# Spreading the four indirect transfers of a block over events of the turn, and holding the gathers of two phases to four blocks ahead

## The reference

```python
x = layernorm(x + gcn(x, src, dst, ...))        # two convolutions, 64 -> 128 -> 64
x = layernorm(x + attention(x, src, dst, ...))  # softmax over the edges of a target
x = layernorm(x + relations(x, edge_attr_64, edge_type_10, src, dst, ...))  # tanh scores, softmax
x = layernorm(x + messages(x, src, dst, edge_attr_32, ...))  # two MLPs
# e.g. attention:
#   e = gelu(s_src[src] + s_dst[dst]);  a = softmax of e over the edges of one dst
#   h = segment_sum(a * z[src], dst) + (x @ res_W + res_b)
```

## Time and profile before

| | us |
|---|---|
| median of 3 runs | 6235.68 |
| lowest, highest | 6197.13, 6236.36 |
| the profiled execution, its own time | 6214.3 |
| its span, first to last instruction | 6212.5 |

### The profile page before, as it was taken

The page is one execution under the profiler, slowest core; times in us unless marked ns, Lnnn a source line. Parts: engine busy times, 40 slices in busy tenths (PEclk is TensorE's granted clock), DMA queues, the critical chain, the costliest instruction groups (busy, mean ns, idle before and its releaser), DMA issues. The chain is left out here.

```text
span 6212.5 us, 80161 instructions
## 1 busy us (share of the span) xinstructions
PE 5134.0 (83%) x25341; PEld 3285.1 (53%) x25341; DVE 3278.3 (53%) x6838; ACT 1898.0 (31%) x3531; POOL 2770.6 (45%) x2859
## 2 busy tenths in 40 slices
PE   6899988888889999727888789999999877777776
PEld 1266666666667676604555545555555534444443
DVE  9755555555544444526555467777777622222222
ACT  0055554333333333301111114444444311111111
POOL 0144443545544444463542153433332056666665
PEclk9899998899989999956565598888888677777777
DMA  1177776666754454323332243333333122222221
GB/s 31 37 214 218 221 221 190 165 167 174 177 147 136 129 138 133 102 54 82 90 87 73 58 101 82 91 87 90 86 86 78 29 67 54 53 46 52 54 54 24
DMA packets 1124519, 649.11 MB, mean 104 GB/s; under 512 B 907542, under 2 KB 940589, under 8 KB 1124104
## 3 DMA queue, kind: packets, MB, share of 16 engines
q1 hardware_dynamic: 1036296, 555.84, 33.0%
q0 software_dynamic: 87808, 88.16, 7.1%
HBM read 384.69 MB, written 261.63 MB: 104 GB/s over the span
## 5 line engine op out<-in xcount | busy, mean ns | idle before, releaser
L1047 POOL DMA_INDIRECT o_rows<-in_x_dram,dst_idx x392 | 370.0, 944 | 661.8 <-POOLq L347 265.9
L1488 POOL DMA_INDIRECT b_rows<-h_table,slot_idx x392 | 369.8, 943 | 440.9 <-DVE n_res L1021 318.9
L2591 DVE TENSOR_TENSOR_SCAN m_both<-m_keep,m_both,m_rows_t 128x512 f32<-128x512 bf16 x97 | 124.2, 1280 | 815.0 <-remote 458.1
L2464 POOL DMA_INDIRECT out_dram<-s_res,put_out x392 | 390.4, 996 | 352.6 <-DVE s_res L1241 223.9
L1931 POOL DMA_INDIRECT t_got<-x_table,slot_idx x392 | 370.8, 946 | 383.9 <-DVE t_rows L2041 239.7
L1305 POOL DMA_INDIRECT a_got<-node_table,src_idx x392 | 372.0, 949 | 368.5 <-DVE n_res L1021 214.2
L1201 ACT ACTIVATE s_square<-s_sum_t 128x256 f32<-128x256 f32 x392 | 149.2, 381 | 1232.6 <-remote 580.3
L2245 PE MATMUL r_source_t<-r_masked,rel_pair 64*128 64x512 f32 x980 | 523.0, 684 | 0.0
L2247 PE MATMUL r_own_t<-r_masked,rel_pair 64*128 64x512 f32 x980 | 522.8, 684 | 0.0
L1007 DVE TENSOR_REDUCE n_power<-n_square 128x8 f32<-128x512 f32 x294 | 200.9, 683 | 604.9 <-ACT n_square L982 312.0
L2146 POOL DMA_INDIRECT r_got<-x_table,slot_idx x392 | 382.4, 976 | 297.8 <-POOLq L1920 183.0
(11 more groups left out here) (390 smaller groups left out, 13082.2 us busy)
## 6 DMA issues: line engine op xcount, KB each, us to landing
x_table<-n_res SPq DMA_DIRECT2D x196, 256.0 KB
n_rows<-x_table SPq DMA_DIRECT2D x196, 256.0 KB
x_table<-s_res SPq DMA_DIRECT2D x294, 128.0 KB
node_table<-n_wide SPq DMA_DIRECT2D x98, 272.0 KB
h_table<-n_conv SPq DMA_DIRECT2D x98, 256.0 KB
x_table<-s_res SPq DMA_DIRECT2D x98, 256.0 KB
r_feats<-in_edge_attr_dram SPq DMA_DIRECT2D x390, 64.0 KB
n_rows<-in_x_dram SPq DMA_DIRECT2D x97, 256.0 KB
```

The source lines that it names most:

```text
L1047: nc.gpsimd.indirect_dma_start(out=rows[:, n % 4, t, :], out_offset=None, in_=x, in_offset=bass.IndirectOffsetOnAxis(ap=dst_idx[:, n * TIL ...
L1488: nc.gpsimd.indirect_dma_start(out=rows[:, n % 4, t, 0:D], out_offset=None, in_=h_table, in_offset=bass.IndirectOffsetOnAxis(ap=slot_idx[: ...
L2464: nc.gpsimd.indirect_dma_start(out=out, out_offset=bass.IndirectOffsetOnAxis(ap=put_out[:, n * TILES + t:n * TILES + t + 1], axis=0), in_= ...
```

## The change

In the first five phases each of a block's four gathers now waits for an event of its own. In the attention and relation phases `gather(n)` also waits for `scanned[n - 4]` before its first transfer, so that it no longer runs ahead over the whole ring. Nothing is computed otherwise, and the number of transfers is the same.

```diff
 own_phase, gather(n), in the loop over t:
-                            if t == TILES // 2 and n >= 5:
+                            if t == 1 and n >= 8:
+                                pool.wait_ge(fed.powered[n - 8], fed.powered.done(n - 8))
+                            if t == 2 and n >= 8:
+                                pool.wait_ge(fed.ready[n - 8], fed.ready.done(n - 8))
+                            if t == 3 and n >= 5:
                                 pool.wait_ge(nodes.ready[n - 5], nodes.ready.done(n - 5))
 first_conv_phase:
-                            if t == TILES // 2 and n >= 5:
+                            if t == 1 and n >= 6:
+                                pool.wait_ge(conv_made[n - 6], conv_made.done(n - 6))
+                            if t == 2 and n >= 5:
                                 pool.wait_ge(nodes.ready[n - 5], nodes.ready.done(n - 5))
+                            if t == 3 and n >= 4:
+                                pool.wait_ge(scanned[n - 4], scanned.done(n - 4))
 second_conv_phase:
-                            if t == TILES // 2 and n >= 4:
+                            if t == 1 and n >= 4:
+                                pool.wait_ge(nodes.powered[n - 4], nodes.powered.done(n - 4))
+                            if t == 2 and n >= 4:
                                 pool.wait_ge(nodes.ready[n - 4], nodes.ready.done(n - 4))
+                            if t == 3 and n >= 4:
+                                pool.wait_ge(norm.ready[n - 4], norm.ready.done(n - 4))
 attention_phase:
+                        if n >= 4:
+                            pool.wait_ge(scanned[n - 4], scanned.done(n - 4))
                         for t in range(TILES):
+                            if t == 1 and n >= 4:
+                                pool.wait_ge(source_matched[n - 4], source_matched.done(n - 4))
+                            if t == 2 and n >= 4:
+                                pool.wait_ge(score_kept[n - 4], score_kept.done(n - 4))
+                            if t == 3 and n >= 4:
+                                pool.wait_ge(turned[n - 3], turned.done(n - 3))
 relation_phase:
+                        if n >= 4:
+                            pool.wait_ge(scanned[n - 4], scanned.done(n - 4))
                         for t in range(TILES):
+                            if t == 1 and n >= 4:
+                                pool.wait_ge(masks_made[n - 4], masks_made.part(n - 4, 1))
+                            if t == 2 and n >= 4:
+                                pool.wait_ge(masks_made[n - 4], masks_made.done(n - 4))
```

## The result

The changed kernel takes 5974.94 us (median of 4 runs, 5966.95 to 5996.67), the kernel before 6218.20 us beside it (4 runs, 6197.13 to 6236.36): a ratio of 0.9631, with a 95% interval of 0.9599 to 0.9663. The forecast was 6180 with a range down to 6085; the kernel gained 243 us where 56 were forecast. The profiled execution has a span of 5980.8 us against 6212.5.

What follows compares the result with a forecast made beforehand. It took PE to bound own phase, convolutions and relations, and PE's signals, late during POOL's long gather runs, to hold attention. Gains of 45 + 6 + 5 = 56 us gave 6180 from 6235.7; 8 in 10 between 6085 and 6255.

Steps and rivals of the forecast that it cites:

- The reading: All phases: while POOL issues many gathers back to back, PE's finished work reaches others late, some 21 us at attention's start.
- The first rival: Attention's start: the late signal has nothing to do with POOL's run, the change only reorders POOL; 6236 us, chance 0.17.
- own phase and convolutions: First three phases: gathers stay nearly one run of four in an undisturbed turn; counted as 0 for all three.
- the runs of eight: Eight gathers of POOL in one run: expected rarer in attention, about as frequent in the first convolution.
- the sum: Whole kernel: 45 + 6 + 5 = 56 us off, from a median of 6235.7 to 6180, 0.9% faster.
- Attention, start: Up to block 28: POOL tied to the turn, turns of 6.0 us between 5.0 and 7.0; 45 us gained, 20 to 70.
- my own list: Signs in the changed profile; wrong would be, among others, turns of 7 us and more at attention's start.
- Attention, later: Rest of attention: the fourth gather's wait stops runs of two blocks; 6 us gained, between 0 and 18.
- Relations: Relations: first run about 22 gathers instead of 28, 5 us gained; later product hidden by 3.3 us slack, early turns 0.
- Small gaps are enough: First convolution: single gathers with any gap never delay PE's signals, 118 us more gained; 6062 us, chance 0.20.
- The long pause is what counts: Second convolution: cutting POOL's 3.3 us pause into pieces costs 108 us, turns above 8.3 us; 6288 us, chance 0.13.

Runs made afterwards that it cites:

- the probe: Kernel before; in attention's first 12 turns ACT makes a one-column activation as it sees each of four signals (rows landed, PE's work counted); 6209.59 us.
- the pause experiments: Kernel before with POOL memsets of different lengths between indirect transfers; the 128x256 one, about 0.2 us more per transfer, took 5897.46 us, ratio 0.9593.
- e3_parts: Kernel before with the change's waits in own phase, waits for long past events in first convolution, only the scanned[n - 4] hold in attention and relations; ratio 0.9765.
- the pauses: Kernel before with its own waits and a POOL memset of 128x512 between a block's transfers, in attention and relations before every transfer; 5856.72 us, ratio 0.9486.
- the two runs of 903 and 974 us: Changed kernel with all events awaited before a block's first transfer (ratio 1.018); kernel before with a 128x512 memset pause after every second transfer (1.0051).
- g2_pairs: Kernel before with a POOL memset of 128x512 only after every second indirect transfer, message phase included; 6238.23 us, ratio 1.0051.

## Why the prediction was wrong

**The reading was right, as far as it went.** "While POOL issues many gathers back to back, what PE has finished reaches the others late": the probe shows it with PE's two kinds of signal, and pausing POOL alone removes it. The first rival, that the late signal has nothing to do with the run, is out.

**The step that failed** is that of own phase and convolutions: the four events of a turn are "each little more than the 1.24 us apart that POOL needs for one. So in an undisturbed turn it is still nearly one run of four", and hence 0. The term measured 82 us in own phase, 44 in the first convolution and 8 in the second. The sentence was worked out for the first convolution and carried over to own phase unread. In own phase it is false: 144 gathers stand alone and 16 runs of four are left of 55, and 66 increments in place of 183 are over 1 us late. I asked whether the run becomes much looser, not how loose it has to be. Little is enough: 0.35 to 0.95 us between the gathers in the changed own phase, and in the pause experiments 0.2 us more from transfer to transfer in the message phase. For own phase the change's waits alone give it (715), and without the spread it is gone (821). In the first convolution the sentence is nearly true: half of the distances within a block are 1.29 us or less, and as many signals are late as before. What did change is that the runs of eight, which I had said stay, went from 11 to 1 and those of six from 11 to 35, and that the longest delays are rarer. How much of the 44 us that explains is not shown; waits that never wait gave 20 there (e3_parts). I had also looked for the disturbance only in the first convolution; for own phase, with PE busy for 717 of 803 us, I called the turn PE's and looked no further. 86 idle us, at a clock below full, were all to be had: with the pauses 12 are left.

**The clock was missing from the sum.** I had priced a late signal as waiting time. In own phase 38 of the 82 us are matmuls that became shorter (717 to 679 busy, clock 0.91 to 0.95). That less waiting brings a higher clock is no rule, though: in the second convolution the change brought idle time down from 75 to 33 us and busy time up from 736 to 770 (clock 0.96 to 0.91), so that 8 us are left; and in the two runs of 903 and 974 us PE idles for 66 and 78 us, as before, at 0.83 and 0.78. What sets the clock in these phases stays open.

**Attention, start**: forecast 45, measured 57, within the bounds of 20 and 70. The turn to block 28 is 158.7 / 28 = 5.7 us on the mean, between the bounds of 5.0 and 7.0 and near the 6.0 that I took. That it came so near is partly luck: the picture was one block of gathers a turn and turns of 6, and what came was runs of 15 to 18 gathers and turns between 2.2 and 14.7 us, as PE's signals are still late in every longer run. By my own list turns of 7 us and more were a sign of being wrong. **Attention, later**: forecast 6 with a bound of 18, measured 35. Blocks 28 to 90 gained 17 (7.53 to 7.25 us a turn), which the bound holds. Another 18 lie in the last stretch, from block 90's sum to the phase's last (191.4 to 173.4); but the probe's kernel, with the waits of before, took 175.8 there, so I do not put these down to the change.

**Relations**: forecast 5, measured 3, within what one execution can tell; the first run has 22 gathers, as worked out. The product comes 6.1 us after the masks begin (forecast 5.4 later than 0.4, so 5.8), and 3.05 us of slack are left (forecast 3.3). This was the step read most closely, and it came out, but for the early turns: there `match` does wait for the product, 14 times and for 12 us together. I had allowed up to 5 us for that; the phase as a whole hides it.

**The rivals.** "Small gaps are enough" was the nearest, with 0.20. Its price, 118 us for the first convolution, is nearly what the pauses give there (735 to 629, 106); the change gives 44, since in the fast turns POOL does run through, as I said: 35 runs of six and one of eight are left. But I had priced the rival for that phase alone, as if the mechanism stopped at its door. With the 82 us of own phase in it, it would have come to 6236 - 56 - 118 - 82 = 5980, and that this is the measured time would have been luck: 74 us too much in the first convolution against 41 too little in attention and 8 in the second, from a median that lay 18 us higher. "The long pause is what counts" had a second convolution above 8.3 us a turn; it is 8.2. With the pause in another place the same phase is at 9.9, but not by that rival's mechanism, since hardly any signal is late there.

## What to carry to other kernels

When a wait ends late on an engine whose record says it was done, and another engine issues indirect transfers all the while, put a short pause between the transfers before anything else: it costs four lines, shows in one profile whether the two belong together, and here half a microsecond was worth more than a hand-picked event for each transfer. If a mechanism is seen in one phase, price it in all phases, and ask how little of a cure is enough, not only how much the edit brings. And where PE is the bound at a clock below full, read the granted clock of each phase before and after: it gave own phase 38 us more than the waiting alone, and took 34 from the second convolution.

## What the runs showed of the hardware

PE's signals reach ACT, DVE and SP up to 29 us late while POOL issues indirect transfers 1.25 us apart; DVE's signal reaches PE in 0.06 us at the same time. In the first convolution of the kernel before, what PE finishes during the first two transfers of a run is not late (15 cases, DVE's sums and ACT's copies). What it finishes during the third holds DVE's sum up by 2.2 us on the mean (14 cases), and during the tenth, in the message phase, by 10.8 us (11 cases). It is not the length of the run so far that counts alone: in the message phase's runs of sixteen the increments whose work ended during the ninth to fifteenth transfer are seen 2.7 us on the mean after the last transfer of the run has ended (85 increments, 1.2 to 3.1), so that those of the ninth are 11.5 us late and those of the fifteenth 4.7. At 1.49 us from transfer to transfer nearly none is late in the message phase; at 1.45 within a block and 1.25 between blocks 228 of 450 still are in the first convolution. Memsets that keep POOL as busy do not cause it. The Trainium skill (TensorE: Matmul & The Clock Gate, "The cost: per-tile semaphore tail") says that PE's increments are written one after another and puts one at about 26 ns; the order fits, the probe's two came 9.85 us apart. Why POOL's indirect transfers should slow them, and whether only indirect ones do, no run here shows.

TensorE's clock can make a small difference large: in the second convolution of g2_pairs turns of 8.4 us at full clock, with PE idle for 13% of the time, alternate with turns of 12.9 us at 0.58 of it, in which PE hardly idles. In the kernel before the turns of 8.0 us, with PE idle for 7 to 9%, stay at a clock of 0.96 to 1.00 from 1911 us to the phase's end. What decides between the two no run shows.
